# ScalarE copies the attention's context and sums out of their PSUM bank; VectorE divides in SBUF; four engine orders rewritten

## The reference, cut to what matters

```python
def sdpa(q, k, v, causal):
    scale = 1.0 / np.sqrt(q.shape[-1])
    scores = jnp.einsum('bhqd,bhkd->bhqk', q * scale, k)
    ...
    p = jax.nn.softmax(scores.astype(jnp.float32), axis=-1).astype(q.dtype)
    return jnp.einsum('bhqk,bhkd->bhqd', p, v)
```

## Time and profile before

| | |
|---|---|
| median of 3 runs | 1376.25 us (1374.81 to 1379.65) |
| the profiled execution's own time | 1375.08 us |
| its span, first to last instruction | 1372.8 us |
| PE / PEld busy | 1306.5 (95%) / 1055.0 us (77%) |
| DVE busy | 761.5 us (55%) |
| ACT busy | 467.8 us (34%) |
| POOL busy | 457.3 us (33%) |
| mean granted TensorE clock | 0.978 of full speed |
| chain that ended last, by engine | PE 81%; DVE 6%; POOL 5%; ACT 4%; issue 3% |

### The profile page before, as it was taken

One profiled execution on the slowest core, in us unless ns is written; L12 is line 12 of the kernel. 1 busy time (PEld: TensorE's weight loads), 2 busy tenths in 40 slices (PEclk: granted clock), 3 DMA queues, 4 the chain that ended last, 5 costly groups with the idle time before them and its releaser, 6 DMA issues.

```text
span 1372.8 us, 25897 instructions
## 1 busy us (share of the span) xinstructions
PE 1306.5 (95%) x10931; PEld 1055.0 (77%) x10931; DVE 761.5 (55%) x1361; ACT 467.8 (34%) x779; POOL 457.3 (33%) x559
## 2 busy tenths in 40 slices
PE   7898899999999999999999999998899999999988
PEld 5775677877877778888888888876578777787766
DVE  2645666656656756444344553345566657576553
ACT  3333234324233133243344434433442332423321
POOL 1232444435434433311111211224444254344332
PEclk9787899999999999999999999999999999999999
DMA  9001000000001001120000000011000000000000
GB/s 321 12 2 61 2 2 2 1 2 2 1 2 47 1 5 43 44 72 1 0 1 1 1 0 1 1 42 42 1 2 1 2 17 1 2 17 2 1 16 16
DMA packets 19900, 27.28 MB, mean 20 GB/s; under 512 B 3432, under 2 KB 15552, under 8 KB 19520
## 3 DMA queue, kind: packets, MB, share of 16 engines
q1 hardware_dynamic: 19008, 24.20, 5.3%
q10 hardware_dynamic: 768, 1.26, 0.3%
HBM read 23.35 MB, written 2.10 MB: 19 GB/s over the span
## 4 chain that ended last, share of the span: by engine, by line
PE 81%; DVE 6%; POOL 5%; ACT 4%; issue 3%; ACTq 0%; DVEq 0%; POOLq 0%
PE bank L956 5%; PE bank L1100 5%; PE bank L1246 5%; PE bank L1211 4%; PE row_banks L1360 4%; PE bank L1216 4%; PE bank L1420 4%; PE bank L1463 4%; PE bank L1456 4%; PE row_banks L1083 4%; PE row_banks L1050 3%; PE bank L1235 3%; PE bank L949 2%; PE bank L1018 2%; PE bank L1221 2%
## 5 line engine op out<-in xcount | busy, mean ns | idle before, releaser
L1816 DVE TENSOR_REDUCE room<-row_banks 128x4 f32<-128x512 f32 (+1 forms) x128 | 116.5, 952 | 24.8 <-PE row_banks L1055 24.4
L806 POOL TENSOR_SCALAR_AFFINE_SELECT room<-room 128x1024 f32<-128x1024 f32 x64 | 70.4, 1103 | 167.6 <-ACT room L1574 167.6
L1574 ACT ACTIVATE room<-row_banks 128x1536 f32<-128x1536 f32 x64 | 93.0, 1452 | 81.7 <-PE row_banks L1083 81.6
L1246 PE MATMUL bank<-room,down_w 128*128 128x256 f32 x384 | 94.0, 384 | 0.5 <-DVE room L1916 0.5
L1606 ACT ACTIVATE room<-bank 128x256 f32<-128x256 f32 x96 | 36.4, 383 | 134.9 <-PE bank L1216 125.6
L1246 PEld LDWEIGHTS bank<-room,down_w 128*128 128x128 f32 x384 | 69.6, 190 | 12.3 <-issue 3.3
L1830 DVE RECIPROCAL room<-bank 128x256 f32<-128x256 f32 x32 | 56.1, 1754 | 39.3 <-PE bank L1100 39.2
L768 POOL TENSOR_TENSOR room<-room 128x256 f32<-128x256 f32 x32 | 24.7, 772 | 157.7 <-ACT room L1586 157.7
L1586 ACT ACTIVATE room<-x_all 128x512 f32<-128x512 f32 x32 | 20.2, 630 | 151.9 <-DVE x_all L1885 93.8
L1083 PE MATMUL row_banks<-room 32*128 32x256 f32 (+1 forms) x1024 | 62.8, 360 | 7.8 <-ACT room L1574 4.0
L1899 DVE SCALAR_TENSOR_TENSOR room<-room,bank 128x256 f32<-128x256 f32 x96 | 39.9, 416 | 53.3 <-ACT room L1606 53.2
(11 more groups left out here) (243 smaller groups left out, 3043.4 us busy)
## 6 DMA issues: line engine op xcount, KB each, us to landing
out_x<-wq SPq DMA_DIRECT2D x8, 256.0 KB, 2.3
qkv<-in_L_xattn_v_qkv SPq DMA_DIRECT2D x2, 768.0 KB, 5.9
qkv<-in_L_xattn_l_qkv SPq DMA_DIRECT2D x2, 768.0 KB, 8.9
gate_w<-in_L_xattn_v_gate SPq DMA_DIRECT2D x2, 640.0 KB, 8.6
gate_w<-in_L_xattn_l_gate SPq DMA_DIRECT2D x2, 640.0 KB, 7.5
up_w<-in_L_xattn_v_up SPq DMA_DIRECT2D x2, 640.0 KB, 6.0
up_w<-in_L_xattn_l_up SPq DMA_DIRECT2D x2, 640.0 KB, 6.3
down_w<-in_L_xattn_v_down SPq DMA_DIRECT2D x2, 640.0 KB, 6.4
```

Of the source, the lines that this page charges most:

```text
L806: pool.affine_select(out=diagonal, in_=diagonal, compare_op=ALU.is_ge, fill=0.0, base=0, pattern=[[0, 8], [1, P]], channel_multiplier=-1)\
L1246: return pe.matmul(ff_bank[0][:, t * S:(t + 1) * S], down_w[:, f, t * P:(t + 1) * P], hid[:, i, :], start=(i == t == 0), stop=(i == UPS - ...
L1574: act.activation(probs[w % 2], row_banks[:, :, 0:3 * P], ACT.Exp).then_inc(*ATT_ACT.does(e, f"exp{w}"))
L1816: last = dve.tensor_reduce(dst, row_banks[:, :, P * i:P + S * i], X, ALU.max, negate=True)
```

## The change

A new ScalarE stage `values_out(e, t)` copies the whole bank (128x512) to SBUF as soon as `values` has filled it. `context` reads that copy: the reciprocal is written over the sums in SBUF, and the multiplication has both inputs in SBUF. PE's waits for the bank go to the copy (`co0`, `co1`) where they went to VectorE's `ctx0`, `ctx1`. `recip` is gone, `c_ctx` shares the room of `c_recip`, and the two copies live in `a_p[3]` (shared with layer 2) and in new room. All four lists of `ORDER` are replaced; but for the 32 new words on ACT they hold the same words in another order.

```diff
-... "context": ("att", "dve", "rec# ctx#"),
+... "values_out": ("att", "act", "co#"), "context": ("att", "dve", "rec# ctx#"),
...
-        recip, c_q, c_recip, c_ctx = (take(S) for _ in range(4))
+        c_q, c_recip = (take(S) for _ in range(2))
+        c_ctx = c_recip
+        ctx_raw = [a_p[3], take(TT * S)]
...
# n0_sum, for e % B > 2; a_center of e == 0 in the same way with e - 3 -> B - 1
-                        pe.wait_ge(*ATT_DVE.did(e - 3, "ctx1"))
+                        pe.wait_ge(*ATT_ACT.did(e - 3, "co1"))
# turn_max
-                        pe.wait_ge(*ATT_DVE.did(e - 1, "ctx1"))
+                        pe.wait_ge(*ATT_ACT.did(e - 1, "co1"))
# values, w == 2
-                        pe.wait_ge(*ATT_DVE.did(e, "ctx0"))
+                        pe.wait_ge(*ATT_ACT.did(e, "co0"))
...
+                def values_out(e, t):
+                    act.wait_ge(*ATT_PE.did(e, f"pv{2 * t + 1}"))
+                    if e > 0:
+                        act.wait_ge(*ATT_DVE.did(e - 1, f"ctx{t}"))
+                    act.copy(ctx_raw[t], att_bank[:]).then_inc(*ATT_ACT.does(e, f"co{t}"))
...
                 def context(e, t):
-                    dve.wait_ge(*ATT_PE.did(e, f"pv{2 * t + 1}"))
+                    dve.wait_ge(*ATT_ACT.did(e, f"co{t}"))
                     if e > 0 and t == 0:
                         dve.wait_ge(*ATT_POOL.did(e - 1, "cl"))
-                    dve.reciprocal(recip, att_bank[:, S:2 * S]).then_inc(*ATT_DVE.does(e, f"rec{t}"))
+                    dve.reciprocal(ctx_raw[t][:, S:2 * S], ctx_raw[t][:, S:2 * S]).then_inc(*ATT_DVE.does(e, f"rec{t}"))
                     dve.wait_ge(*ATT_DVE.did(e, f"rec{t}"))
-                    dve.tensor_tensor(ctx_sb[:, t, :], att_bank[:, 0:S], recip, ALU.mult).then_inc(*ATT_DVE.does(e, f"ctx{t}"))
+                    dve.tensor_tensor(ctx_sb[:, t, :], ctx_raw[t][:, 0:S], ctx_raw[t][:, S:2 * S], ALU.mult).then_inc(*ATT_DVE.does(e, f"ctx{t}"))
```

Of the orders, the stretches that the prediction speaks of (minus before, plus after):

```diff
# pe, element 0
-        second_scores.0.3 first_scores.1.0 values.0.2 values.0.3
+        second_scores.0.3 values.0.2 first_scores.1.0 values.0.3
# pe, element 9
-        second_scores.9.3 cross_second.8 values.9.2 cross_values.8 values.9.3 cross_project.8 first_scores.10.0 crs_sum.8.1 v.11
+        second_scores.9.3 values.9.2 cross_second.8 values.9.3 cross_values.8 v.11 cross_project.8 first_scores.10.0 crs_sum.8.1
# pe, element 1: the same words on both sides
         second_scores.1.3 cross_second.0 values.1.2 cross_values.0 values.1.3
# pe, element 15
-        up.14.0 crs_sum.15.0 crs_spread.15.0 up.14.1 cross_q.15
+        up.14.0 crs_sum.15.0 up.14.1 crs_spread.15.0 up.14.2 cross_q.15
# act, element 9 (values_out.e.0 stands within two words of exp.e.3 in every element, ahead of it in 12 of 16)
-        exp.9.2 k_out.11 q_out.11 exp.9.3 cross_exp.8
+        exp.9.2 values_out.9.0 exp.9.3 q_out.11 cross_exp.8 values_out.9.1 k_out.11
# dve, layer 0
-        f_shift.3 f_gated.2 f_sums.3 f_gated.1 f_mean.2 p_seen.0 f_gated.0 f_mean.1 f_gated.3
+        f_shift.3 f_sums.3 p_seen.0 f_gated.2 f_gated.1 f_gated.0 f_mean.1 f_mean.2 f_gated.3
# pe, layer 0
-        f_gate.2 f_gate.1 f_turn.3 f_context.3 f_sum.2 f_gate.0 f_spread.2 f_gate.3 f_sum.1
+        f_turn.3 f_gate.2 f_gate.1 f_context.3 f_gate.0 f_gate.3 f_sum.1 f_sum.2 f_sum.0 f_spread.1
# act, layer 2: changes between b_gelu and a_exp in the list
-        24
+        28
```

More of the change, by code:

```diff
@@ L187 @@
         first_scores.2.2 up.0.0 n0_sum.4 crs_sum.1.0 first_scores.2.3 crs_spread.1.0 up.0.1 cross_q.1 n0_spread.4
[L188 to L191, removed]
+        cross_first.1 up.0.2 turn_max.2 up.0.3 second_scores.2.0 up.0.4 second_scores.2.1 values.2.0 second_scores.2.2
@@ L199 @@
[L199 to L203 removed]
+        down.1.0 down.1.1 down.1.2 cross_project.2 late_down.1.0 down.1.3 late_down.1.1 late_down.1.2 crs_sum.2.1
@@ L264 @@
-        values.9.2 cross_values.8 values.9.3 cross_project.8 first_scores.10.0 crs_sum.8.1 v.11 crs_spread.8.1
+        second_scores.6.0 cross_turn_max.5 up.4.4 second_scores.6.1 values.6.0 second_scores.6.2 values.6.1
+        second_scores.6.3 up.4.5 values.6.2 cross_second.5 values.6.3 down.4.0 cross_values.5 down.4.1
+        first_scores.7.0 cross_project.5 down.4.2 down.4.3 crs_sum.5.1 down.4.4 crs_spread.5.1 first_scores.7.1
+        memory.6 down.4.5 dense.6 first_scores.7.2 up.5.0 crs_sum.6.0 up.5.1 up.5.2 crs_spread.6.0 first_scores.7.3
@@ new lines @@
+        first_scores.13.0 down.10.0 down.10.1 cross_project.11 q.14 down.10.2 down.10.3 crs_sum.11.1 v.14
+        crs_spread.11.1 down.10.4 down.10.5 memory.12 first_scores.13.1 k.14 dense.12 up.11.0 n0_sum.15
+        first_scores.13.2 up.11.1 n0_spread.15 crs_sum.12.0 up.11.2 crs_spread.12.0 first_scores.13.3 cross_q.12
+        up.11.3 cross_first.12 turn_max.13 up.11.4 up.11.5 second_scores.13.0 late_up.11.0 second_scores.13.1
+        values.13.0 second_scores.13.2 cross_turn_max.12 values.13.1 second_scores.13.3 late_up.11.1 cross_second.12
@@ new lines @@
+        values.13.2 values.13.3 cross_values.12 down.11.0 down.11.1 late_up.11.2 down.11.2 down.11.3 late_down.11.0
+        cross_project.12 down.11.4 down.11.5 late_down.11.1 late_down.11.2 crs_sum.12.1 turn_out.10 turn_out.11
+        crs_spread.12.1 first_scores.14.0 q.15 memory.13 first_scores.14.1 dense.13 first_scores.14.2 v.15
+        crs_sum.13.0 first_scores.14.3 crs_spread.13.0 k.15 cross_q.13 up.12.0 up.12.1 cross_first.13 up.12.2
+        turn_max.14 up.12.3 second_scores.14.0 up.12.4 second_scores.14.1 cross_turn_max.13 values.14.0
@@ new lines @@
+        second_scores.14.2 values.14.1 second_scores.14.3 up.12.5 cross_second.13 values.14.2 cross_values.13
+        values.14.3 first_scores.15.0 cross_project.13 down.12.0 down.12.1 crs_sum.13.1 down.12.2 down.12.3
+        crs_spread.13.1 first_scores.15.1 down.12.4 memory.14 down.12.5 up.13.0 dense.14 first_scores.15.2 up.13.1
+        crs_sum.14.0 up.13.2 crs_spread.14.0 first_scores.15.3 cross_q.14 up.13.3 cross_first.14 up.13.4 turn_max.15
+        up.13.5 second_scores.15.0 late_up.13.0 second_scores.15.1 cross_turn_max.14 values.15.0 second_scores.15.2
@@ new lines @@
+        late_up.13.1 values.15.1 second_scores.15.3 down.13.0 down.13.1 cross_second.14 down.13.2 values.15.2
+        cross_values.14 values.15.3 late_up.13.2 cross_project.14 down.13.3 down.13.4 down.13.5 crs_sum.14.1
+        late_down.13.0 late_down.13.1 late_down.13.2 crs_spread.14.1 turn_out.13 memory.15 turn_out.12 dense.15
+        up.14.0 crs_sum.15.0 up.14.1 crs_spread.15.0 up.14.2 cross_q.15 cross_first.15 up.14.3 cross_turn_max.15
+        up.14.4 cross_second.15 up.14.5 cross_values.15 down.14.0 cross_project.15 down.14.1 crs_sum.15.1 down.14.2
```

578 lines of the change are left out of this document (281 added, 297 removed).

## The result

The changed kernel takes 1353.03 us (1352.2 to 1357.66) where the kernel before, run beside it, takes 1377.53: a ratio of 0.983, 95% interval 0.9801 to 0.986. That is 24.5 us less; forecast were 7.7, and the range ended at 1360. The direction was right, the size was not.

A forecast was written before the change was run, and what follows sets the result against it. TensorE, busy 1306.5 of 1372.8 us, bounds the kernel, so gains come through its 66.3 us idle time or the clock. -1.6 - 2.6 - 1.0 - 2.5 = -7.7 us gives a forecast of 1368.6 us, range 1360 to 1380.

The forecast's parts named there:

- layer 0: p_seen moved ahead of f_gated.2 into a 9.0 us VectorE hole: -2.5 us; up to 8.5 us of clock, 0 taken.
- Removing the wait alone: TensorE nowhere waits for the bank under the old order, so the earlier free bank alone is worth 0.
- four table loads: Layer 2: ScalarE changes between GELU and exp four times more, 1.283 us each; 0 taken, +5.1 us the other end.
- the two stalls': TensorE idle 1.86 us before 46.26 and 2.09 us before 53.11, both said to hang on p_seen.
- rival 2: Clock lost after the first layer's idle time and in one short later stretch comes back too: about 1363 us, chance 0.14.
- second stretch: Short stretch at the lower clock after 150, in layer 1's fill: 1.7 us that could come back.
- Element 9: values.9.2, values.9.3 and v.11 fill TensorE gaps at cross_second.8, cross_values.8 and cross_project.8, 3.24 us in all: -2.6 us.
- Element 0: values.0.2 fills TensorE's 1.65 us of idle time before first_scores.1.0: -1.6 us.
- The tail: A tile of up.14 fills TensorE's 1.04 us wait for GpSimd before crs_spread.15.0: -1.0 us.
- signs of being wrong: TensorE idle time in the steady part or layer 2 growing over 3 us, or a lower-clock stretch in a new place.
- Rival 3: Context's product delays GpSimd's mask up to 0.42 us in 16 elements, 6.7 us: 1375.3 us, no change, chance 0.24.
- Rival 4: Round 1 copy heading ScalarE's list delays exp 3: 1387 us, near 1381 if a third stay covered; slower, chance 0.18.

The follow-up runs named there:

- e1: Changed code with all 32 copies under the orders of the kernel before: 1394.01 us, ratio 1.0120 to the kernel before.
- e11: Orders of the kernel before with 16 copies, those of round 1 alone, round 3 divided out of the bank: 1378.71 us, ratio 1.0014.
- e3: Kernel before with the changed orders in layer 0 alone: 1367.89 us, ratio 0.9936.
- e5: Changed kernel with the old orders of layer 0 put back: 1366.75 us, ratio 0.9913 to the kernel before.
- second profile: Changed kernel unaltered, profiled again in one of its fastest executions: 1349.23 us, span 1347.3 us.
- e4: Kernel before with one VectorE word moved, p_seen.0 ahead of f_gated.2: 1374.49 us, ratio 0.9970.
- e12: Kernel before with p_seen.0 ahead of f_gated.2 on VectorE and f_square.0 ahead of f_tanh.3 on ScalarE: 1374.08 us, ratio 0.9975.
- e6: Kernel before to the end of layer 2, then changed orders with 16 copies in layer 3: 1369.90 us, ratio 0.9937.
- e2: Code of the kernel before, without copies, under the changed orders: 1372.52 us, ratio 0.9956.
- e16: Kernel before with the changed orders of layer 0, but f_square.0 put back behind f_tanh.3 on ScalarE: 1368.33 us, ratio 0.9933.

## Why the prediction was wrong

**What held.** The bound (TensorE, its idle time and its clock) and most of the places were right: the gain lies in layer 0, at the start of layer 3 and in the tail, and the 315 us of steady layer 1 gave 0.7 us of idle time. The fill of layer 1 gave 0.9 us for the 1.6 forecast. Removing the wait alone is worth nothing (e1, e11). The copy took 0.585 us for the 0.587 forecast, the reciprocal did not move, four table loads came and are hidden: layer 2 has 0.3 us of idle time.

**The term that failed is layer 0**, "Between 0 and the two stalls' 3.95 us I take -2.5 us" and the clock of which "I take 0". The runs have 9 to 15 us there (e3 and e5). Over the whole kernel the sum had 7.7 us, all of it idle time; the profiles have 13.3 to 14.0 us of idle time, and the clock gave 3.1 us more in the slower execution and 12.2 in the faster. In the second profile both stalls are gone, and so are 0.46 and 0.53 us beside them, 4.9 in all; 17 us at half the clock that do not come are 8.5 more; the first exp is 15.2 us early. The mechanism I had as rival 2, and gave 0.14. Its second stretch came back too: it stands at 139.5 to 143 us before (3.5 us, clock 0.51), and not "after 150" as I had it, and neither profile of the changed kernel has one there. Its argument against itself was that "the chain through layer 0 must leave PE idle somewhere": the new list covers that chain almost wholly (0.4 us of idle time from 40 to 52). I never read that list for layer 0 against the chain, word by word, as I did for the elements 0 and 9; and I had the second stall hang on `p_seen`, where e4 and e12 show that `f_square.0` behind `f_tanh.3` holds it.

**Element 9** was priced well: 1.65 before `cross_second.8` and 1.04 before `cross_project.8` are gone, 2.7 against 2.6. **Element 0** gave 1.65 less a new wait of 0.48 for the maximum, 1.2 against 1.6. **The tail** has 1.04 gone, and 1.3 us of idle time less in all. What was not in the sum is the rest of the new layer 3: 1.62 us before `dense.9`, 0.3 of 0.84 at 889.7 us, 0.5 of 1.24 near 954 us, 0.8 twice before tiles of `up`. The start of layer 3 went from 15.5 to 10.4 us where I had 13, and e6 measures about 9 us for layer 3 where the sum had 3.6; its profile has 7.3 us less idle time than before. Each is a small wait that a reordered neighbour fills, and I had costed only the moves that the copy made possible. One of my signs of being wrong did show, a stretch at the lower clock in a new place (967.5 to 975 us), but it cost 3.4 us in a kernel that was faster than forecast.

**Rival 3, the collision.** It happens and is small. The product and `select` in the changed kernel, then in the kernel before:

```profile
1009.71 1.09 POOL L813 TENSOR_SCALAR_AFFINE_SELECT room<-room 128x1024 f32<-128x1024 f32 x1 [1.58 <-ACT room L1581]
1009.73 1.34 DVE L1845 TENSOR_TENSOR room<-room 128x256 f32<-128x256 f32 x1
```

```profile
1190.31 1.09 POOL L806 TENSOR_SCALAR_AFFINE_SELECT room<-room 128x1024 f32<-128x1024 f32 x1 [1.11 <-ACT room L1574]
1190.69 0.42 DVE L1832 TENSOR_TENSOR room<-bank,room 128x256 f32<-128x256 f32 x1
```

With one input in the bank the product runs inside the mask's time and takes its 0.42 us; with both in SBUF it started just behind the mask and took 1.34. Of the 32 products 5 were longer (478, 661, 722, 1343, 1346 ns), 2.4 us in all, half of the 4.8 forecast. Where the product came first, the mask took 1.11 to 1.28 us for 1.09: at most 0.19 us, and not the 0.42 in each of 16 elements that rival 3 needed. By the Trainium skill, page "SBUF — State Buffer", section "Who interferes with whom", a VectorE instruction with one SBUF input (outside its two-port modes) doesn't contend with GpSimd, one with two does with a GpSimd instruction that reads SBUF, and the one that issues second is blocked; both fences agree.

**Rival 4** was right in kind and wrong in its place. In the new orders the copies cost TensorE nothing at the exps: it waits 5.1 us for them before `second_scores`, and 5.1 in e2, which has no copy.

```profile
PE row_banks L1096 <- ACT room L1587: 5.1, 12, 1.7
```

```profile
PE row_banks L1089 <- ACT room L1580: 5.1, 13, 1.7
```

In the old ones (e1) the copies cost 14 us, but mostly through that of round 3, with masks and tanh behind it, and not through the exp behind that of round 1 as I had it (e11: 1 to 2 us).

## What to carry to other kernels

Price the reordering, not only the edit it is sold with: here the old bank under the new orders with three words moved gives all but 2 to 5 us of the change, and the new code under the old order loses 14. A wait that has been short for long can be an instruction queued behind another one's wait; before an idle gap is put down to a cause, name the instruction that ends it and follow its own engine's list one step back. An instruction added to a queue costs the wait that it brings to the head of the queue, so look at what stands behind it.

## What the runs showed of the hardware

The granted clock differs between executions of one kernel, with no difference in its instructions: 0.51 and 1.00 in the same ten microseconds, with TensorE busy in both. Over the whole span it was 0.979 and 0.985, and TensorE's busy time for the same matmuls was 1303.4 and 1294.3 us, which is all of the 8.4 us between the two profiled spans (the idle time was 52.3 and 53.0). That is more than several of the effects studied here. And the two gaps of 1.9 and 2.1 us in layer 0 were followed by 17 us at half the clock, 8.5 us lost, twice their own length; two gaps of 1.46 and 0.51 us (e16) by 3.4 us; around three waits of e2 another 7.9 us went the same way.
